# A graph layer on one core: eight message buffers in the edge stage, and x loaded five and four turns ahead

## The reference

```
h    = concat(x[row], x[col])                      # 25000 x 512
msgs = silu(h @ W1.T + b1) @ W2.T + b2             # 25000 x 256
agg  = segment_sum(msgs, row, N) / (count(row) + 1e-8)
gi   = agg @ w_ih.T + b_ih ;  gh = x @ w_hh.T + b_hh      # N x 768 each
r, z = sigmoid(i_r + h_r), sigmoid(i_z + h_z)
n    = tanh(i_n + r * h_n)
x_new = (1 - z) * n + z * x
y    = gamma * layernorm(x_new) + beta
out  = layernorm(x + y)
```

## Time and profile before

| | us |
|---|---|
| median of 3 runs (2403.91 to 2411.65) | 2405.72 |
| the profiled execution | 2403.31 |
| its span, first to last instruction | 2401.6 |
| TensorE busy | 2185.4 (91%) |
| VectorE busy | 1999.3 (83%) |
| GpSimd busy | 1742.8 (73%) |
| ScalarE busy | 1539.8 (64%) |

### The profile page before, as it was taken

The page is one execution under the profiler, slowest core; times in us unless marked ns, Lnnn a source line. Parts: engine busy times, 40 slices in busy tenths (PEclk is TensorE's granted clock), DMA queues, the critical chain, the costliest instruction groups (busy, mean ns, idle before and its releaser), DMA issues.

```text
span 2401.6 us, 48711 instructions
## 1 busy us (share of the span) xinstructions
PE 2185.4 (91%) x10620; PEld 1667.8 (69%) x10620; DVE 1999.3 (83%) x6515; ACT 1539.8 (64%) x3158; POOL 1742.8 (73%) x1824
## 2 busy tenths in 40 slices
PE   6898998899898989889999999999999999999995
PEld 4777777777777777666666666676676667666763
DVE  6776776667676666669999999999999999999998
ACT  3444444444444444558888888888888888887876
POOL 5656666666666656468888888888888888888885
PEclk9999999999999999989999999999999999999998
DMA  5666666666566656657767677666666676766763
GB/s 159 219 222 211 217 231 211 219 211 227 207 230 217 215 202 215 225 198 227 237 232 227 227 235 238 228 236 222 228 231 228 230 235 226 239 232 224 234 215 131
DMA packets 206647, 528.22 MB, mean 220 GB/s; under 512 B 58696, under 2 KB 67680, under 8 KB 206608
## 3 DMA queue, kind: packets, MB, share of 16 engines
q1 hardware_dynamic: 124168, 320.62, 38.3%
q0 software_dynamic: 81600, 206.79, 26.9%
q10 hardware_dynamic: 840, 0.40, 0.1%
HBM read 475.46 MB, written 207.08 MB: 284 GB/s over the span
## 4 chain that ended last, share of the span: by engine, by line
PE 26%; DVE 24%; issue 19%; DMA 12%; POOL 8%; another core or an unknown queue 7%; ACT 2%; DVEq 1%; POOLq 0%; SPq 0%; ACTq 0%
PE banks L1086 23%; DMA mg<-messages,rows_now 11%; DVE tg L1028 4%; POOL mg L391 4%; DVE st L1064 3%; DVE uu L1039 3%; PE banks L1102 3%; DVE diff L1011 3%; DVE oh L990 2%; DVE zd L1016 2%; POOL xb L515 1%; DVE msg L779 1%; DMA xts<-in_xt 1%; POOL rs L531 1%
## 5 line engine op out<-in xcount | busy, mean ns | idle before, releaser
L1086 PE MATMUL banks<-whh,xts 128*128 128x512 f32 (+1 forms) x1568 | 561.5, 486 | 0.0
L391 POOL DMA_INDIRECT mg<-messages,rows_now x392 | 449.9, 1148 | 94.4 <-issue 86.0
L1086 PE MATMUL banks<-mg,oh 128*128 128x512 f32 (+1 forms) x1568 | 322.4, 348 | 78.3 <-DVE npre L1005 50.3
L587 ACT ACTIVATE msg<-banks 128x512 fp32r<-128x512 f32 (+1 forms) x392 | 187.0, 493 | 321.6 <-PE banks L1086 174.9
L1086 PEld LDWEIGHTS banks<-mg,oh 128*128 128x128 f32 x1568 | 253.3, 189 | 182.9 <-issue 128.1
L1086 PEld LDWEIGHTS banks<-whh,xts 128*128 128x128 f32 x1568 | 269.4, 189 | 151.8 <-issue 141.4
L391 POOL DMA_INDIRECT xsrc<-in_x,src_now x196 | 192.1, 980 | 243.4 <-PE banks L1102 113.6
L1086 PE MATMUL banks<-wsh,silh 128*128 128x512 f32 (+1 forms) x784 | 278.7, 356 | 80.8 <-DVE msg L779 77.2
L658 ACT ACTIVATE banks<-banks,rcount 128x768 f32<-128x768 f32 x392 | 326.5, 871 | 27.9 <-PE banks L1086 16.6
L779 DVE TENSOR_TENSOR msg<-banks,msg 128x512 fp32r<-128x512 f32 (+1 forms) x392 | 203.9, 552 | 163.5 <-ACT msg L587 129.1
L1086 PE MATMUL banks<-wsl,silh 128*128 128x512 f32 (+1 forms) x784 | 273.8, 349 | 0.0
(11 more groups left out here) (139 smaller groups left out, 5495.4 us busy)
## 6 DMA issues: line engine op xcount, KB each, us to landing
messages<-msg SPq DMA_DIRECT2D x196, 772.0 KB
xts<-in_xt SPq DMA_DIRECT2D x196, 256.0 KB
xs<-in_x SPq DMA_DIRECT2D x196, 256.0 KB
out_y<-yy SPq DMA_DIRECT2D x196, 256.0 KB
near<-tile_blocks SPq DMA_DIRECT2D x49, 128.0 KB
mg<-messages,rows_now POOLq DMA_INDIRECT x392
xsrc<-in_x,src_now POOLq DMA_INDIRECT x196
xdst<-in_x,dst_now POOLq DMA_INDIRECT x196
```

The lines of the kernel that those rows point to most:

```text
L391: nc.gpsimd.indirect_dma_start(out=dst_tile, out_offset=None, in_=rows, in_offset=bass.IndirectOffsetOnAxis(ap=table, axis=0), bounds_chec ...
L587: nc.scalar.activation(msg[:, u % EU, n0:n1], p_g[:, part, 0:n1 - n0], ACT.Copy).then_inc(e_gh[part], 1)
L1086: return nc.tensor.matmul(out_, lhsT, rhs, start=start, stop=stop, skip_group_check=skip)
```

## The change

Edge stage: EU goes from 4 to 8, so a message buffer is written again after eight tiles; the waits for `e_stored` count accordingly. The two semaphores of the x gathers (`got_src`, `got_dst`) become one (`got_xe`, waited for at 32), those of the two SiLU results too (`e_sh`).

Node stage: xs and xts have XQ = 8 buffers. x^T is loaded five turns ahead, x four. Both additionally wait until the segment sum of the pair AHEAD = 5 before is done (`n_sg1`); the waits for the readers of a buffer now look eight pairs back. The two gathers of a pair raise one semaphore (`got_m[u % QU]`), which the one-hots of both blocks await at its full count.

Memory: `before`, `put` and the slot table's scratch now share memory with message rows 6 and 7 or others, and some tiles stand in another order. In the branch that isn't taken VectorE waits for the stores first. The turn index u now runs to 8, so that tiles with four buffers are indexed by u % QU; those lines are left out here.

```diff
-EU = 4
+EU = 8
+XQ = UNROLL
...
-        before, put = sb("before", [P, ROW], f32r, until=early), sb("put", [P, ROW], f32r, until=early)
...
+        apart = ExitStack()
+        sb("rows_below", [P, EU - 2, ROW], until=apart)
+        before, put = sb("before", [P, ROW], f32r, until=apart), sb("put", [P, ROW], f32r, until=apart)
+        apart.close()
...
         msg = sb("msg", [P, EU, ROW], f32r, until=early)
...
-        xs, xts = sb("xs", [P, QU, 2 * D]), sb("xts", [P, QU, 2 * D])
+        xs, xts = sb("xs", [P, XQ, 2 * D]), sb("xts", [P, XQ, 2 * D])
...
-        got_src, got_dst, e_stored = sems("got_src", XE), sems("got_dst", XE), sems("e_stored", EU)
+        got_xe, e_stored = sems("got_xe", XE), sems("e_stored", EU)
...
+            AHEAD = 5
+
             def load_counts(q, u):
                 need(sp, S["n_sg1"], q - QU + 1)
...
             def load_x(q, u):
-                need(sp, S["n_xl"], q - QU + 1)
-                need(sp, S["n_mm"], q - QU + 1)
+
+                need_apart(sp, sp_passed, S["n_sg1"], q - AHEAD + 1)
+                need(sp, S["n_xl"], q - XQ + 1)
+                need(sp, S["n_mm"], q - XQ + 1)
...
             def load_rows(q, u):
-                need(sp, S["n_diff"], q - QU + 1)
-                need(sp, S["n_xb"], q - QU + 1)
+                need_apart(sp, sp_passed, S["n_sg1"], q - AHEAD + 1)
+                need(sp, S["n_diff"], q - XQ + 1)
+                need(sp, S["n_xb"], q - XQ + 1)
...
-            node_turns(sp, ((store_y, -8), (load_counts, 3), (load_x, 3), (load_rows, 2)), first=-4, last=8)
+            node_turns(sp, ((store_y, -8), (load_counts, 3), (load_x, 5), (load_rows, 4)), first=-5, last=8)
...
-                            gather(to, rows_now[:, 2 * u + h:2 * u + h + 1], messages, got_m[2 * u + h], last_row)
+                            gather(to, rows_now[:, u % QU * 2 + h:u % QU * 2 + h + 1], messages, got_m[u % QU], last_row)
...
-                need(act, e_stored[u % EU], 16 * quad(g, u))
+                need(act, e_stored[u % EU], 16 * g)
...
-                    dve.wait_ge(got_m[2 * u + h], 16 * (nth(q, u) + 1))
-                    last = nc.vector.tensor_scalar(oh[0:SLOTS, u, h, :], iota1[0:SLOTS, :],
+                    dve.wait_ge(got_m[u % QU], 32 * (nth(q, u) + 1))
+                    last = nc.vector.tensor_scalar(oh[0:SLOTS, u % QU, h, :], iota1[0:SLOTS, :],
...
-                pe.wait_ge(got_src[u % XE], 16 * nth_)
-                pe.wait_ge(got_dst[u % XE], 16 * nth_)
+                pe.wait_ge(got_xe[u % XE], 32 * nth_)
```

More of the change, by code:

```diff
@@ L245, in edge_slots, with nth @@
                     also(n)
-        def nth(q, u):
-            return (q if isinstance(q, int) else q - u) // QU + (0 if isinstance(q, int) else u // QU)
+        def nth(q, u, buffers=QU):
+            return q // buffers if isinstance(q, int) else (q - u) // buffers + u // buffers
         def duo(q, u):
@@ L257, in step @@
                     if not isinstance(q, int) or 0 <= q + lag < PAIRS:
-                        part(q + lag, (u + lag) % QU)
+                        part(q + lag, (u + lag) % UNROLL)
             head = UNROLL * (-(min(lag for _, lag in parts) // UNROLL) + 1)
@@ L420, in indices @@
                 for u in range(XE):
-                    need(pool, got_dst[u], 16 * (n + (-1)))
+                    need(pool, got_xe[u], 32 * (n + (-1)))
                 nc.gpsimd.tensor_copy(src_now[:, side, :], srci[:, bass.ds(n * XE, XE)]).then_inc(idx_now, 1)
@@ L481, in _ @@
             for u in range(EU):
-                pool.wait_ge(e_stored[u], 16 * (TILES // EU))
+                pool.wait_ge(e_stored[u], 16 * len(range(u, TILES, EU)))
             def node_stage(summed):
@@ L508, in x_lo @@
                     need(pool, S["n_mm"], q - QU + 1)
-                    nc.gpsimd.tensor_tensor(out=xl[:, u, :], in0=xts[:, u, D:2 * D], in1=xh[:, u, :].bitcast(f32),
+                    nc.gpsimd.tensor_tensor(out=xl[:, u % QU, :], in0=xts[:, u, D:2 * D], in1=xh[:, u % QU, :].bitcast(f32),
                                             op=ALU.subtract).then_inc(S["n_xl"], 1)
@@ L638, in x_hi @@
             def x_hi(q, u):
-                act.wait_ge(got_xt[u], 16 * (nth(q, u) + 1))
+                act.wait_ge(got_xt[u], 16 * (nth(q, u, XQ) + 1))
                 need(act, S["n_mm"], q - QU + 1)
-                nc.scalar.activation(xh[:, u, :], xts[:, u, D:2 * D], ACT.Copy).then_inc(S["n_xh"], 1)
+                nc.scalar.activation(xh[:, u % QU, :], xts[:, u, D:2 * D], ACT.Copy).then_inc(S["n_xh"], 1)
             def gates(q, u, h):
@@ L667, in last_norm @@
                 act.wait_ge(S["n_nmr"], q + 1)
-                need(act, n_stored[u], 16 * nth(q, u))
+                need(act, n_stored[u % QU], 16 * nth(q, u))
                 for h in range(2):
-                    last = nc.scalar.activation(yy[:, u, h * D:(h + 1) * D], uu[:, u, h * D:(h + 1) * D],
-                                                ACT.Identity, bias=nmr[:, u, h:h + 1], scale=rs2[:, u, h:h + 1])
+                    last = nc.scalar.activation(yy[:, u % QU, h * D:(h + 1) * D], uu[:, u % QU, h * D:(h + 1) * D],
+                                                ACT.Identity, bias=nmr[:, u % QU, h:h + 1], scale=rs2[:, u % QU, h:h + 1])
                 last.then_inc(S["n_y"], 1)
@@ L768, in edge_silu_lo @@
                 k, side = quad(g, u), u // QUAD
[L769 to L770 removed]
+                dve.wait_ge(e_sh[m], k * 2 + 2)
                 need(dve, e_g[1], k * QUAD - QUAD)
@@ L782, in edge_local @@
             def edge_local(g, u):
-                need(dve, e_stored[u % EU], 16 * quad(g, u))
+                need(dve, e_stored[u % EU], 16 * g)
                 nc.vector.tensor_copy(msg[:, u % EU, LOC:LOC + 1], locf[:, bass.ds(slot(g, u), 1)]).then_inc(e_loc, 1)
@@ L921, in _ @@
             with dve.If(n_levels > 1):
+                for u in range(EU):
+                    dve.wait_ge(e_stored[u], 16 * len(range(u, TILES, EU)))
                 nc.vector.memset(put[:, :].bitcast(f32), 0.0).then_inc(v_zero, 1)
@@ L1063, in stats1 @@
                 for h in range(2):
-                    last = nc.vector.bn_stats(st1[:, u, h, :], xn[:, u, h * D:(h + 1) * D])
+                    last = nc.vector.bn_stats(st1[:, u % QU, h, :], xn[:, u % QU, h * D:(h + 1) * D])
                 last.then_inc(S["n_s1"], 1)
@@ L1069, in aggregate1 @@
                 for h in range(2):
-                    last = nc.vector.bn_aggr(ag1[:, u, h, :], st1[:, u, h, :])
+                    last = nc.vector.bn_aggr(ag1[:, u % QU, h, :], st1[:, u % QU, h, :])
                 last.then_inc(S["n_a1"], 1)
@@ L1120, in edge_hidden @@
                     pe.wait_ge(e_lo, k * QUAD + QUAD)
-                    need(pe, e_sh[m], k)
+                    need(pe, e_sh[m], k * 2)
                 o = p_hid[:, m, :]
@@ L1241, in with_x @@
                         else:
-                            hi, lo = (t[:, u, c * P:(c + 1) * P] for t in (xh, xl))
+                            hi, lo = (t[:, u % QU, c * P:(c + 1) * P] for t in (xh, xl))
                             mm(to, hi, wxh[:, c, n0:n1], False, False, True)
```

94 lines of the change are left out of this document (48 added, 46 removed).

## The result

The changed kernel takes 2369.11 us (median of 4 runs, 2361.75 to 2370.72) where the kernel before took 2404.81 beside it (4 runs, 2399.23 to 2411.65): ratio 0.9844, 95% interval 0.9811 to 0.9877.

A forecast was written before the change was run, and what follows sets the result against it. It took TensorE and VectorE, both nearly full in the node stage, and TensorE, busy 860.80 of 950 us in the edge stage, as bounds. 2403.3 + 0 - 9 + 6.5 + 0.5 = 2401.3, forecast 2404 us on the median's scale, range 2382 to 2424.

The forecast's parts named there:

- Edge stage, 0 us for eight message buffers: Edge stage: doubling the message buffers removes no wait, since they come free long before they are asked for; 0 us.
- SyncE waits for ScalarE, the burst goes out some 2 us earlier: Node stage: SyncE loses its wait for x + beta, so output, x^T and x start with their middle 2.2 us earlier.
- Bound of 29.5 us for the late waits, of which 30% go: Node stage: VectorE's waits for gathered message rows total 29.5 us over 196 turns; 30% of them vanish, -9 us.
- The half of the engines that the gathers need is full all the time: Node stage: gathers and burst fill half the DMA engines for 6.9 us of a 6.86 us turn, so moving the burst gains little.
- no gain and 2415 us: Node stage: by engines taking turns between queues, nothing is gained and the merged gather wait costs +9; counted in C.
- One semaphore for both gathers, +6.5 us: Node stage: the first one-hot also waits for the second gather, 0.27 us in each of 24 late turns; +6.5 us.
- Start of the node stage, +0.5 us: Node stage start: nine loads instead of seven precede SyncE's first wait, delaying the first gathers; +0.5 us, at most 1.4.
- B: Node stage rival: gathers come free of the burst, half to all late waits go; 2377 to 2396 us, chance 0.29 with D.
- C: Node stage rival: the earlier burst delays the older second gather, more turns become late; 2420 us, chance 0.27.
- D: Edge stage rival: message buffers matter after all, -50 us at most, 2356 us; small chance, counted within B's 0.29.
- fewer than 10 late turns: Node stage sign that the forecast is wrong and B holds: under 10 turns in which VectorE waits for gathers.
- The 20 to 30 waits at the first one-hot: Node stage sign that the forecast is right: VectorE's gather waits move to the first one-hot, 20 to 30 in 1200 us.

The follow-up runs named there:

- before_slots_by_4: The kernel before with message slots reordered so that partition 4m + r takes slot 32r + m, burst in its old place; 2236.52 us, ratio 0.9849.
- the first order: The kernel before with message slots reordered so that partition 8j + i takes slot 16i + j, burst in its old place; 2269.95 us, ratio 0.9996.

## Why the prediction was wrong, step by step

**Edge stage, 0 us for eight message buffers: right.** The "remote" waits stayed at 92.0 and 103.4 us, and the ratio without the eight buffers is 0.9842, with them 0.9834, well within the intervals. On chip 8 the stage ends at the same 880 us in both. The 7.6 us by which it ended sooner in the first pair of profiles is open: one profile each, on a chip whose "remote" waits the profile does not explain; it isn't the buffers as far as the other chips can tell.

**SyncE waits for ScalarE, the burst goes out some 2 us earlier: right.** By the timeline the output and x^T leave 2.6 us sooner against the pair, x 0.3 us. SyncE waits for ScalarE, and ScalarE's waits for x^T are gone, as the signs of being right had it.

**Bound of 29.5 us for the late waits, of which 30% go: the step that failed.** All went; the turns got shorter by 34.5 us in all on the first chip and by 33.0 on chip 8, where -9 was forecast. The late waits themselves were 30.5 us over all the turns on the first chip and 29.8 on chip 8, so the bound was sized rightly; what was wrong is the share of it, and so the passage "The half of the engines that the gathers need is full all the time. Then moving the burst changes who goes first, and not when the sum is done: what the younger pair gains, the older gather pays."

- That gathers alone keep the DMA share at one half was right, and `before_slots_by_4` shows that this limit is what makes them late beside the burst. For the 0.50, though, eight partitions in a row per engine was the wrong reason: it would have spread the first order over all 16. Groups of four are the rule that the two orders fit.
- That this half is *full* was an average made into a law. Its work is 3.7 + 2.05 = 5.75 us (with 786,432 bytes for the 768 KB 2.1, and 5.8) in a turn of 6.86. The 1.2 that brought it to 6.9 is the measured share over what the bare transfers would need. But the share adds up the times of packets, and these overlap: up to 22 are at work at once on the 16 engines. So it doesn't say how full an engine is. The changed kernel shows it: there 0.69 x 6.68 = 4.6 us a turn make a factor of 1.18, and by the same sum the half is again filled for longer than the turn (6.8 of 6.68 us), yet no gather is late. And there are stretches with gathers in flight in which the share is below even one half, in the trace of before too. One of before (a pair of gathers was issued at 1618.25 and 1619.91, the next began at 1625.67), then two of the changed kernel:

```profile
1625.00:1627.00 2.00, 1.54 (x9) 1.40 (x10) 1.97 (x9) 1.58 (x3) 1.78 (x2) 1.00 0.47 114
```

```profile
1607.00:1608.00 1.00, 1.00 (x9) 0.92 (x8) 1.00 (x3) 1.00 (x4) 0.99 (x3) 1.00 0.40 111
1608.00:1609.00 1.00, 1.00 (x6) 0.52 (x5) 1.00 (x4) 1.00 (x4) 0.72 (x1) 1.00 0.42 167
```

Of the 1200 stretches of one us from 1100 to 2300, 182 are below 0.50 before and 163 after. There was room in both; what changed is where the burst lies.

- That someone among the gathers must pay overlooked the third party. x and x^T are wanted turns later; if they wait, nobody does. The number of packets at work at once, in the mean over 160 turns of the two profiles of chip 8, shows how it went. From 3 to 5 us after a pair's first gather SyncE's queue has 5.0 at work beside 6.6 of the gathers before the change (x^T, which takes 6.2 us to land); after it, 0.5 beside 8.3. The older gather is not through when the burst comes at -2.0: it still has some 8 at work when those of the output start, a good 5 us after its own pair's first gather. But it ends no later: from 1 to 2 us after the younger pair's first gather 0.9 of its packets are left at work, where 3.8 were before.

The Trainium skill, "DMA: Bandwidth & Descriptors", section "Queues, rings and completion order", has each engine take turns between its queues, and from that rule the prediction made no gain and 2415 us. The run has 2369.11. The rule says how one engine shares its time while both queues have work; whether both have work at once is what the change altered, and the rule is silent on that.

**One semaphore for both gathers, +6.5 us: the price right, the count wrong.** In the kernel before alone, 0.27 us for each late wait was to give +12 us with 46 of them, +10 with the 38 of that chip, and +13 was measured (+8 to +18 by the interval). With no late turn the term is 0.

**Start of the node stage, +0.5 us: right in size**, +1.0 on the first chip, +0.5 on chip 8 (31.2 and 31.7 us from the last message to the first `npre`).

**Rivals.** B put 2377 to 2396 us; measured 2369.11, and 2361.75 in the profiled run. That lies below even its far end by 8 to 15 us: 5 us are turns that got shorter beyond the waits of the earlier trace rows (34.5 against 29.5), of which some 4 are VectorE's own busy time for a turn (6.60 and 6.57 us; why is open), 7.6 the open part of the edge stage. C, the older gather pays, is refuted for this place of the burst. That a burst lying on a gather makes it late is true, but it is the pair issued just ahead of the burst or with it that pays. D, the message buffers, is refuted.

**The signs named beforehand**: fewer than 10 late turns was to mean B, and there are none; the median turn was to stay, and it did (6.71 and 6.69). The 20 to 30 waits at the first one-hot that were to show the forecast right did not come.

## What to carry over

When a bulk transfer and one that an engine waits for meet in every turn, do not reason from the mean load: lay both on one turn's time axis, find the gap, and see which of them has turns to spare; here 0.3 to 2.6 us in a turn of 6.7 were worth 1.6%, and one wait instruction or one lag number sets it. A measured DMA share is no evidence that a resource is full: it was 0.70 with the late gathers and 0.69 without them. Compare the bare demands (5.75 of 6.86 us) instead, and look for stretches in which the share falls. And where a gather is mostly empty rows, look at which partitions the used rows fill: two orders of the same rows gave shares of at most 0.65 and of 0.89 in the stretches shown, and the second hid the collision but for one late wait of 0.6 us.

## What the runs showed of the hardware

- Gathers alone into partitions 0 to 63 keep the DMA share at 0.50; rows spread by eights give 0.65 at most in the stretch shown, rows spread by fours 0.89. The time between gathers falls from 1.87 us to between 1.1 and 1.4.
- With the rows spread by fours x and the output land in 2.8 and 2.9 us instead of 3.6 and 4.2 though they leave at the same places, so the direct transfers had been slowed as well as the gathers.
- Two chips differ by 5.9% on the same kernel (2404.81 us, and 2270.46 on chip 14), nearly all of it in the edge stage: 133 us to the last message on chip 8, while turns of the node stage agree to 0.2% (6.854 and 6.843). On the slower one GpSimd has 95 us of edge-stage waits whose releaser the profile can't name, and ScalarE 97 before its message copies and 107 elsewhere; on the others there are none. What they are is open.
